# Down projection's low parts on VectorE; dt, products and norm steps moved in a Mamba-2 layer with two MLPs

## The reference

```python
x = hidden                                    # 2 x 512 x 512, float32
x = layernorm(x + attn(x)); x = layernorm(x + ffn(x))

def attn(x):                                  # res + mamba, then res + mlp
    h = x + mamba2(rmsnorm(x, ln1_w))
    h2 = rmsnorm(h, ln2_w)
    return h + (silu(h2 @ gate_w.T) * (h2 @ up_w.T)) @ down_w.T      # 1792 wide

def mamba2(x):                                # 4 heads of 128, state 128, chunks of 128
    z, xs, Bs, Cs, dt = split(x @ w_in.T)
    xs, Bs, Cs = silu(causal_conv4(xs, Bs, Cs) + conv_b)
    dt = softplus(dt + dt_bias); cs = cumsum(-dt * exp(A_log))       # per chunk
    y = ((C B^T) * exp(cs_q - cs_k) [lower]) (x dt) + C S_prev exp(cs) + D x
    return (y * silu(z)) @ w_out.T            # S is carried from chunk to chunk

def ffn(x):                                   # 1376 wide, ternary weights
    q(w) = round(clip(w / (mean|w| + 1e-5), -1, 1)) * mean|w|
    return ((x @ q(w_gate).T) * (x @ q(w_up).T)) @ q(w_down).T
```

## Time and profile before

| | before |
|---|---|
| median of three executions | 504.51 us |
| profiled execution, its own time | 506.52 us |
| its span, first to last instruction | 504.7 us |
| PE busy | 478.6 us (95%) |
| PEld busy | 380.0 us (75%) |
| DVE busy | 322.3 us (64%) |
| ACT busy | 236.7 us (47%) |
| POOL busy | 273.8 us (54%) |
| mean granted TensorE clock | 0.987 |
| chain that ended last | PE 76%, DVE 9%, POOL 6%, issue 4%, ACT 3% |

### The profile page before, as it was taken

One profiled execution on the slowest core, in us unless ns is written; L12 is line 12 of the kernel. 1 busy time (PEld: TensorE's weight loads), 2 busy tenths in 40 slices (PEclk: granted clock), 3 DMA queues, 4 the chain that ended last, 5 costly groups with the idle time before them and its releaser, 6 DMA issues.

```text
span 504.7 us, 6223 instructions
## 1 busy us (share of the span) xinstructions
PE 478.6 (95%) x2104; PEld 380.0 (75%) x2104; DVE 322.3 (64%) x482; ACT 236.7 (47%) x444; POOL 273.8 (54%) x278
## 2 busy tenths in 40 slices
PE   8999999979898989999999979999989999999995
PEld 8886677767576768788788757788868888888884
DVE  3785786643777856677998879994955722421233
ACT  5869767665556666455342333333905441023200
POOL 5726475443852586766877588954703432233421
PEclk9999999998999999999999989999999999999999
DMA  7522021022202415342332145330210000100002
GB/s 247 199 98 85 1 84 62 21 64 77 88 25 83 151 58 188 127 172 82 123 125 99 47 150 204 126 125 1 84 63 0 1 0 1 62 23 0 2 6 77
DMA packets 14431, 40.80 MB, mean 81 GB/s; under 512 B 2368, under 2 KB 2368, under 8 KB 14400
## 3 DMA queue, kind: packets, MB, share of 16 engines
q1 hardware_dynamic: 14400, 40.41, 23.1%
HBM read 38.30 MB, written 2.10 MB: 80 GB/s over the span
## 4 chain that ended last, share of the span: by engine, by line
PE 76%; DVE 9%; POOL 6%; issue 4%; ACT 3%; DMA 2%; POOLq 0%; SPq 0%; DVEq 0%; ACTq 0%
PE psA L1609 8%; PE psA L1610 8%; PE psA L1398 6%; PE psA L1400 6%; PE psB L1619 4%; PE psB L1618 4%; PE psA L1404 3%; PE psA L1406 3%; PE psA L1584 3%; PE psA L1588 3%; PE psA L1587 3%; DVE xbc L1175 2%; PE psA L1386 2%; PE psA L1391 2%; PE psA L1387 2%
## 5 line engine op out<-in xcount | busy, mean ns | idle before, releaser
L1609 PE MATMUL psA<-xT_h,q_gu 128*128 128x512 f32 x176 | 70.2, 399 | 1.5 <-DVE x L1330 1.5
L1610 PE MATMUL psA<-xT_l,q_gu 128*128 128x512 f32 x176 | 69.1, 393 | 0.0
L823 POOL TENSOR_TENSOR int_l<-prod_t,int_h 128x512 fp32r<-128x512 f32 x22 | 28.5, 1297 | 59.3 <-ACT int_h L1043 59.2
L1350 DVE TENSOR_TENSOR prod_t<-gate_t,psA 128x512 f32<-128x512 f32 x22 | 15.2, 689 | 54.5 <-PE psA L1610 49.4
L717 POOL TENSOR_TENSOR beta<-wsum,beta 128x512 fp32r<-128x512 f32 x28 | 36.0, 1308 | 25.5 <-ACT beta L899 25.5
L1038 ACT ACTIVATE gate_t<-psA 128x512 f32<-128x512 f32 x22 | 13.1, 597 | 76.9 <-PE psA L1610 76.9
L765 POOL TENSOR_TENSOR act_hl<-act,act_hl 128x512 fp32r<-128x512 f32 x28 | 42.2, 1527 | 9.1 <-ACT act_hl L1017 9.1
L1609 PEld LDWEIGHTS psA<-xT_h,q_gu 128*128 128x128 f32 x176 | 33.1, 188 | 10.1 <-issue 2.0
L1319 DVE SCALAR_TENSOR_TENSOR q<-raw,scl,qtmp 128x512 fp8e4<-128x512 f32 x33 | 39.8, 1205 | 1.2
L1610 PEld LDWEIGHTS psA<-xT_l,q_gu 128*128 128x128 f32 x176 | 33.1, 188 | 7.3
L1317 DVE TENSOR_SCALAR qtmp<-raw,scl 128x512 bf16<-128x512 f32 x33 | 33.2, 1005 | 3.1 <-DMA raw<-in_f_gu_t 3.1
(11 more groups left out here) (251 smaller groups left out, 1391.6 us busy)
## 6 DMA issues: line engine op xcount, KB each, us to landing
raw<-in_f_gu_t SPq DMA_DIRECT2D x22, 512.0 KB, 3.4
raw<-in_w_gu_t SPq DMA_DIRECT2D x14, 512.0 KB, 3.8
raw<-in_f_dn_t SPq DMA_DIRECT2D x10, 512.0 KB, 3.2
raw<-in_w_gu_t SPq DMA_DIRECT2D x14, 256.0 KB, 2.7
raw<-in_w_dn_t SPq DMA_DIRECT2D x7, 512.0 KB, 3.3
raw<-in_w_in_t SPq DMA_DIRECT2D x5, 512.0 KB, 4.3
x<-in_hidden SPq DMA_DIRECT2D x8, 256.0 KB, 5.4
out<-x SPq DMA_DIRECT2D x8, 256.0 KB, 2.0
```

The source lines that it names most:

```text
L1609: nc.tensor.matmul(ps, w, seq(xT_h, k, b), start=k == 0, stop=False)
L1610: done = nc.tensor.matmul(ps, w, seq(xT_l, k, b), start=False, stop=k == KD - 1)
```

## The change

- All low parts of the down projection, `act` and `dn`, are made on VectorE; GpSimd has none of them. The dn loads get counters of their own (`dnh_ready`, `dnl_ready`).
- Input projection of batch 0: `dtturn` stands behind the convolution of tile 5 instead of tile 3, and `until` of the first chunk one tile later.
- Scan of batch 1: p1(0) stands behind `state` and `chunk`; p2(2) and p2(4) stand between the transposes of a chunk and the output projection of the next; p1(9) stands ahead of the last chunk's transposes.
- Second MLP, batch 0: four `ln1a` instead of two stand ahead of the first `ffn`, and the pairs behind them move up by one tile.

```diff
@@ -82,7 +82,7 @@
         steps += before + [("inproj", 0, j)]
         if j in (0, 2):
             steps.append(load("in", 3 + j // 2))
-        if j == 5:
+        if j == 6:
             steps.append(("until", 0, 0))
         if 1 <= j <= NC:
             steps.append(("turn1", NC + j - 1))
@@ -95,7 +95,7 @@
         if j == NX + NZ - 1:
             steps.append(("dtturn", 1))
         steps += after + [("conv", 0, j)] + last
-        if j == 3:
+        if j == 5:
             steps.append(("dtturn", 0))
 
     sums = [("sumgu", f) for f in range(FF)] + [("sumdn", p) for p in range(FF // 2 + 1)]
@@ -125,9 +125,14 @@
         first, second = [("p1", s)], [("p2", s - 1)] if s >= 1 else []
         turned = [c for kind, *_, c in after if kind == "turn2"]
         if s == NX + NZ - 1:
-            steps += before + after + first + [("thigh", NC - 1), ("tlow", NC - 1)] + second + [("gsplit", 0)]
+            steps += before + first + after + [("thigh", NC - 1), ("tlow", NC - 1)] + second + [("gsplit", 0)]
         elif s == SCAN_ACT:
             steps += before + second + after + first + last
+        elif s == 0:
+            steps += before + after + first + last
+        elif turned and s < NX + NZ - 3:
+            steps += before + first + [("turn2", 1, *turned), ("thigh", *turned)] + second
+            steps += [step for step in after if step[0] != "turn2"] + [("tlow", *turned)] + last
         else:
             steps += before + first
             for step in after:
@@ -220,8 +225,9 @@
     for b in range(NB):
         for f in range(FF):
             if b == 0:
-                steps += between[:2]
-                between = between[2:]
+                now = 4 if f == 0 else 2
+                steps += between[:now]
+                between = between[now:]
             steps.append(("ffn", b, f))
             if b == 0 and f in (1, 2, 3, 5, 7, 9):
                 steps.append(("qcvdn", dn_wide.pop(0)))
@@ -253,7 +259,7 @@
 KEEP_WARM = {1: 11, 2: 8, 3: 9}
 IN_ON_DVE = 2
 INPROJ = [n for n, w in enumerate(LOADS) if w[0] == "in"]
-SPLITS = [n for n, w in enumerate(LOADS) if w[0] in ("out", "dn")]
+SPLITS = [n for n, w in enumerate(LOADS) if w[0] == "out"]
 PRODUCTS = [s for s in SCHEDULE if s[0] in ("p1", "p2", "p3", "p4", "p5", "p6", "p7")]
 
 
@@ -453,6 +459,8 @@
         silu0_ready = sem("silu0_ready")
         qcv_ready = sem("qcv_ready")
         qdn_ready = sem("qdn_ready")
+        dnh_ready = sem("dnh_ready")
+        dnl_ready = sem("dnl_ready")
         sum_ready = sem("sum_ready")
         tern_ready = sem("tern_ready")
         bn_ready = sem("bn_ready")
@@ -585,8 +593,10 @@
         def raw_used(n):
 
             kind, *at = LOADS[n]
-            if kind in ("out", "dn"):
+            if kind == "out":
                 return [(low_ready, SPLITS.index(n) + 1)]
+            if kind == "dn":
+                return [(dnl_ready, at[0] + 1)]
             if kind == "in":
                 return [in_split(INPROJ.index(n))]
             if kind == "ga":
@@ -747,23 +757,6 @@
                     raw_arrived(pool, n)
                     nc.gpsimd.tensor_tensor(low, raw[:, n % RAW_SLOTS, :], high.bitcast(F32), ALU.subtract)\
                         .then_inc(low_ready, 1)
-                elif kind == "load" and LOADS[at[0]][0] == "dn":
-
-                    n = at[0]
-                    pool.wait_ge(high_ready, SPLITS.index(n) + 1)
-                    raw_arrived(pool, n)
-                    for cols, high, low in dn_parts(LOADS[n][1]):
-                        last = nc.gpsimd.tensor_tensor(low, by_tile(raw[:, n % RAW_SLOTS, cols]), high.bitcast(F32),
-                                                       ALU.subtract)
-                    last.then_inc(low_ready, 1)
-                elif kind == "act":
-
-                    b, f = at
-                    n = FM * b + f
-                    pool.wait_ge(acth_ready, n + 1)
-                    high, low = act_hl[:, n % ACT_SLOTS, 0, :], act_hl[:, n % ACT_SLOTS, 1, :]
-                    nc.gpsimd.tensor_tensor(low, act[:, f, b, :], high.bitcast(F32), ALU.subtract)\
-                        .then_inc(actl_ready, 1)
                 elif kind == "load" and LOADS[at[0]][0] == "gb":
                     weight_sums(at[0])
                 elif kind == "gsplit":
@@ -850,7 +843,7 @@
                     s.wait_ge(*dn_place_free(LOADS[n][1]))
                     for cols, high, _ in dn_parts(LOADS[n][1]):
                         last = nc.scalar.activation(high, by_tile(raw[:, n % RAW_SLOTS, cols]), ACT.Copy)
-                    last.then_inc(high_ready, 1)
+                    last.then_inc(dnh_ready, 1)
                 elif kind == "load" and LOADS[at[0]][0] in ("sumgu", "sumdn"):
 
                     n = at[0]
@@ -1302,6 +1295,23 @@
                     link(nc.vector.tensor_scalar(scl[:, 9:12], scl[:, 6:9], -1.0, None, ALU.mult))
                     link(nc.vector.tensor_tensor(scl[:, 12:13], scl[:, 3:4], scl[:, 4:5], ALU.mult))
                     link(nc.vector.tensor_tensor(scl[:, 13:14], scl[:, 12:13], scl[:, 5:6], ALU.mult))
+                elif kind == "load" and LOADS[at[0]][0] == "dn":
+
+                    n = at[0]
+                    v.wait_ge(dnh_ready, LOADS[n][1] + 1)
+                    raw_arrived(v, n)
+                    for cols, high, low in dn_parts(LOADS[n][1]):
+                        last = nc.vector.tensor_tensor(low, by_tile(raw[:, n % RAW_SLOTS, cols]), high.bitcast(F32),
+                                                       ALU.subtract)
+                    last.then_inc(dnl_ready, 1)
+                elif kind == "act":
+
+                    b, f = at
+                    n = FM * b + f
+                    v.wait_ge(acth_ready, n + 1)
+                    high, low = act_hl[:, n % ACT_SLOTS, 0, :], act_hl[:, n % ACT_SLOTS, 1, :]
+                    nc.vector.tensor_tensor(low, act[:, f, b, :], high.bitcast(F32), ALU.subtract)\
+                        .then_inc(actl_ready, 1)
                 elif kind == "quant":
 
                     (what, f), half = at
@@ -1573,7 +1583,7 @@
                 elif kind == "down":
                     b, f = at
                     n = FM * b + f
-                    pe.wait_ge(high_ready, split_count("dn", f // 2))
+                    pe.wait_ge(dnh_ready, f // 2 + 1)
                     pe.wait_ge(actl_ready, n + 1)
                     high, low = dn_tile(f)
                     act_high = [act_hl[:, n % ACT_SLOTS, 0, chunk(c)] for c in range(NC)]
@@ -1583,7 +1593,7 @@
                         ps = bank_of(job) if f else open_a(job) if b else open_b(job)
                         nc.tensor.matmul(ps, act_high[c], high, start=f == 0, stop=False)
                         if c == 0:
-                            pe.wait_ge(low_ready, split_count("dn", f // 2))
+                            pe.wait_ge(dnl_ready, f // 2 + 1)
                         nc.tensor.matmul(ps, act_high[c], low, start=False, stop=False)
                         last = nc.tensor.matmul(ps, act_low[c], high, start=False, stop=f == FM - 1)
                         if f == FM - 1:
```

## The result

| | before | after |
|---|---|---|
| median of four executions each | 504.61 us (504.22 to 505.97) | 496.16 us (495.74 to 497.11) |
| profiled execution, span | 506.52, 504.7 us | 495.74, 494.0 us |
| PE, DVE, POOL busy | 478.6, 322.3, 273.8 us | 472.2, 318.7, 215.5 us |
| mean granted TensorE clock | 0.987 | 0.996 |

The ratio is 0.983 (95% interval 0.981 to 0.985): 8.4 us faster, where 10 were forecast (494.5). Three later sets had 506.0 to 506.2 us before; in one of them the change was run again: 496.88, ratio 0.982 (0.980 to 0.985). Between the two profiled executions the span shrank by 10.7 us.

What follows compares the result with a forecast made beforehand. TensorE, busy 478.6 of 504.7 us, was taken as the bound, with its waits and half-clock stages removable. Terms +0.5 -5.4 -3.5 -1.5 = -9.9 us gave 494.5 us, range 491.5 to 497.5 (0.66).

Steps and rivals of the forecast that it cites:

- part 2: Scan of batch 1: reordered products remove TensorE waits and half-clock stages, less some waits given back; -5.4 us.
- part 3: Down projection: low parts on VectorE remove 6.3 us of waits and clock loss, new waits cost 2.8; -3.5 us.
- Part 1: Input projection: later dt replaces a 1.2 us wait on a convolution's bank by 1.7 on a silu; +0.5 us.
- chunk 0's turn: Scan of batch 1: waits on the norm (0.4 us) and decay (1.6) go, with a half-clock stage (1.7).
- given back in chunk 2 (+0.9): Scan of batch 1: the output projection ends 1.4 us closer to seg, which waits for VectorE's state sum; +0.9 us.
- The two new waits: Start of the down projection: 1.4 us each at the last tile's p4 and the first down tile's fourth column group.
- Part 4: Start of the second MLP: the third bank is freed while the first product runs, removing a wait; -1.5 us.
- the three stages: Half-clock stretches behind three long waits, two in the scan, one in the down projection: 1.7 us each, all gone.
- the first rival: Ahead of the scan and around the first down tile, new waits drop the clock: 498.7 us; chance 0.17.
- The scan kept its time: Rival: in batch 1's scan closed waits reopen at the next step, so no gain there: 500 us; chance 0.08.
- VectorE the bound: Rival: in the down projection slow ternary steps and low parts make TensorE fall behind: 513 us; chance 0.05.
- No new waits at the start of the down projection: Rival, the lucky case: none there and none in the scan's chunks 2 and 3: 490 us; chance 0.03.

Runs made afterwards that it cites:

- p2_back: The changed kernel with p2(2) and p2(4) put back behind the output projections: 497.10 us.
- p1_p9_back: The changed kernel with p1(0) put back ahead of chunk 0's state step and p1(9) behind the last chunk's turn: 498.26 us.
- ln1a_back: The changed kernel with the norm steps ahead of the second MLP as the kernel before had them: 498.37 us.
- change_again: The changed kernel, unaltered, measured again in a later set: 496.88 us.
- ghost: The changed kernel plus unneeded GpSimd subtractions, as many as the kernel before made for low parts in the down projection: 515.35 us.

## Why the prediction was right, and where it was off

The sign, the places and the order of sizes held; 494.5 was forecast and 496.16 measured, 1.7 us or 0.3% off, inside the range. That the sum came out so near is partly luck: from the start of the input projection on, the profiled executions lie 10.2 us apart where 9.9 were forecast, because part 2 fell short by 1.4 and part 3 went over by 1.4. By its own steps:

- **Part 1, +0.5:** +0.54 by the trace, 0.3 when undone alone. The wait on the silu was 1.85 (1.7 forecast). The table loads again take 1.28 with the logarithm's successor at once behind:

```profile
39.70 1.28 ACT L930 ACT_TABLE_LOAD   x1
40.99 0.22 ACT L930 ACTIVATE dtw<-dtw 128x16 f32<-128x16 f32 x1
41.22 1.28 ACT L941 ACT_TABLE_LOAD   x1
42.52 0.60 ACT L941 ACTIVATE sz<-psA 128x512 f32<-128x512 f32 x1
```

  The rule of the Trainium skill (ScalarE: Activation LUTs, "What ACT_TABLE_LOAD costs") that adds a drain to each had its chance of 0.01; the first chunk would have come 2.8 us later than it did. The rows have 1.29 and 1.30 us from a load's start to the work behind it, and nothing else between.
- **Part 2, -5.4:** -4.0. p1(0) was -2.0 (forecast -2.1, though its own terms, 0.6 and 1.7, add up to 2.3), chunk 0's turn -3.5 (-3.7). The term that was mis-sized is "given back in chunk 2 (+0.9)"; seg waited 1.8. That the projection came 1.4 us nearer was right, as p2_back shows (1.8 against 0.4). But I left VectorE's chain, from the start of the residual step to the end of the state sum, at 5.7 us, and it took 6.6 (137.16 to 143.75). The low part of the weight row stood ahead of the state sum in both programs (five low parts stand between, not the four that I counted). Before, GpSimd's residual step was over when it ran:

```profile
142.50 1.73 POOL L810 TENSOR_TENSOR x<-x,nrm 128x512 f32<-128x512 f32 x1
...
145.10 0.68 DVE L1112 TENSOR_TENSOR alpha<-raw,alpha 128x512 fp32r<-128x512 f32 x1
```

  Now the two run side by side, and the low part, from 140.96 on, takes 1.75:

```profile
140.72 1.44 POOL L803 TENSOR_TENSOR x<-x,nrm 128x512 f32<-128x512 f32 x1
```

  It takes 1.75 in p1_p9_back and in p2_back too, so neither of these moves alone brought it there; what did stays open. p2(10) waited 1.69 (forecast 1.4).
- **Part 3, -3.5:** -4.9. The two new waits were 1.24 and 1.21 (1.4 each). Mis-sized was what was removed: I added listed waits, 4.6 us, but each wait costs about 0.25 more on TensorE's starts. Between starts the gaps beyond 0.23 us sum to 5.4, the slower steps behind them to 0.3, and with the clock stage 7.5 us went where I had 6.3. The two new waits cost 3.0 in the same way, and 0.4 more went in the products ahead of them, which I had left out.
- **Part 4, -1.5:** -1.79, the same under-count, shown by ln1a_back.
- **The clock, 5.1 of the 9.9:** the three stages went, as forecast, in the profiled execution. But I took them as certain in the kernel before and as gone in the changed one. The two fences below are windows of the same program in two executions, first after, then change_again (the clock stands behind POOL's figure):

```profile
46.00:50.00 4.00, 4.00 (x17) 2.74 (x15) 1.21 (x3) 3.95 (x6) 2.28 (x2) 1.00 0.25 74
144.00:148.00 4.00, 4.00 (x19) 3.08 (x20) 1.99 (x4) 3.48 (x8) 1.30 (x1) 1.00 0.16 58
```

```profile
46.00:50.00 4.00, 4.00 (x10) 2.64 (x9) 1.05 (x3) 3.69 (x5) 2.00 (x2) 0.57 0.30 90
144.00:148.00 4.00, 3.68 (x10) 2.85 (x11) 2.13 (x4) 2.05 (x5) 1.03 (x1) 0.64 0.20 66
```

  That second execution took 497.60 us against 495.74. So the first rival (new waits drop the clock, 0.17) is not another outcome but what some executions do.
- **The rivals.** The scan kept its time: no, -4.0. VectorE the bound: no, but its mechanism is real and its price right, as ghost showed; what decided was the medians of the earlier trace rows, 482 and 753 ns, as the steps' own durations. No new waits at the start of the down projection: no, there were two of 1.2.
- **From trace to median.** The two profiled executions lie 10.8 us apart, near the sum of 9.9; the medians lie 8.4 and 9.2 apart in the two sets. The profiled execution of before was 2 us above its median, and I carried the full 9.9 over. Part of the remainder is the clock by chance, part the start (below); how much of each the runs don't settle.

## What to carry to other kernels

When two engines' steps get longer in the same stretch, take the shortest or median duration of each as its own, and price the move of work from one to the other with them: silence on one engine can be worth more than its speed. When a step on TensorE is moved, price the waiting engine's queue afresh, since the same step in the same place may now run beside another engine's and take over twice as long; and at a stage's seam check on each queue what an item waits behind, DMAs included. A wait taken from the list of waits costs about 0.25 us more than listed, and a half-clock stage should be entered with a chance and not as a sure term.
